# Layer-0 output stage of a two-layer state-space network: quarter-image pieces in two buffers per scan direction, norm weights folded into the projection, inverse root applied to the projected result

## The reference, cut to what matters

```python
y = ys[:, 0] + ys[:, 2, :, ::-1]                      # rows forward + rows backward
yt = ys[:, 1] + ys[:, 3, :, ::-1]                     # columns forward + columns backward
y = y + swapaxes(yt.reshape(B, 384, W, H), 2, 3).reshape(B, 384, L)
mu, var = y.mean(axis=1), y.var(axis=1)               # over the 384 channels
y = (y - mu) * rsqrt(var + 1e-5) * ln_w + ln_b
out = einsum('bdhw,md->bmhw', y, out_proj_w)          # 384 -> 192, then + x
```

## Time and profile before

| | us |
|---|---|
| median of 3 runs | 30645.63 |
| lowest, highest run | 30641.72, 30652.83 |
| the profiled execution, its own time | 30641.48 |
| its span (first to last instruction) | 30639.7 |
| layer-0 output stage, adds of the first image alone | 115.3 |
| the same, from the first mean of image 0 to that of image 7 | 978.5 |
| the same, last image | 98.0 |

### The profile page before, as it was taken

The page is one execution under the profiler, slowest core; times in us unless marked ns, Lnnn a source line. Parts: engine busy times, 40 slices in busy tenths (PEclk is TensorE's granted clock), DMA queues, the critical chain, the costliest instruction groups (busy, mean ns, idle before and its releaser), DMA issues. The chain is left out here.

```text
span 30639.7 us, 217449 instructions
## 1 busy us (share of the span) xinstructions
PE 24095.3 (79%) x57214; PEld 9165.7 (30%) x57214; DVE 26756.3 (87%) x22439; ACT 16129.4 (53%) x26407; POOL 24333.7 (79%) x10344
## 2 busy tenths in 40 slices
PE   8777777777777777777777777775699888888877
PEld 3222222222222222222222222222244322222222
DVE  8899999999999999999999999995411599999984
ACT  2455555555555555555555555553222455555552
POOL 1699999999999999999999999994100466666652
PEclk9899999999999999999999999998899999999998
DMA  6433333333333333333333333335522444444455
GB/s 208 172 132 134 132 133 134 132 134 130 134 134 133 133 132 133 134 133 133 133 132 134 134 132 134 132 133 199 176 74 74 142 166 165 166 166 167 166 172 184
DMA packets 1141977, 4379.93 MB, mean 143 GB/s; under 512 B 251344, under 2 KB 289248, under 8 KB 775392
## 3 DMA queue, kind: packets, MB, share of 16 engines
q1 hardware_dynamic: 1034832, 4016.81, 36.0%
q10 hardware_dynamic: 105904, 349.22, 3.2%
HBM read 3706.94 MB, written 658.64 MB: 142 GB/s over the span
## 5 line engine op out<-in xcount | busy, mean ns | idle before, releaser
L794 POOL TENSOR_TENSOR s_dbu<-s_du,s_b_sb 128x1536 f32<-128x1536 f32 (+1 forms) x5634 | 19172.1, 3404 | 1463.7 <-DVE s_h L856 1437.5
L856 DVE TENSOR_TENSOR_SCAN s_h<-s_dA,s_state,s_dbu 128x512 f32<-128x512 f32 x15296 | 18641.1, 1264 | 621.8 <-ACT s_dA L721 615.5
L721 ACT ACTIVATE s_dA<-s_delta,s_negA 128x512 f32<-128x512 f32 x15360 | 10325.9, 685 | 6095.6 <-DVE s_h L856 6080.2
L596 PE MATMUL s_y_ps<-s_hc,s_ident 128*128 128x512 f32 x22528 | 10818.9, 603 | 0.6 <-DVE s_hc L866 0.5
L866 DVE TENSOR_TENSOR s_hc<-s_h,s_c_ps 128x1024 f32<-128x1024 f32 x5632 | 6721.1, 1193 | 251.3 <-issue 229.3
L803 POOL TENSOR_TENSOR s_hc_pool<-s_h,s_c_sb 128x512 f32<-128x512 f32 x4096 | 6675.4, 1630 | 1.1 <-DVE s_h L856 0.8
L586 PE MATMUL s_c_ps<-s_bc,s_sel 96*128 96x512 bf16 x7168 | 2556.1, 392 | 4957.8 <-DVE s_hc L866 4953.3
L596 PEld LDWEIGHTS s_y_ps<-s_hc,s_ident 128*128 128x128 f32 x22528 | 4389.9, 195 | 3497.6 <-issue 3189.0
L604 PE MATMUL s_y_ps<-s_hc_pool,s_ident 128*128 128x512 f32 x8192 | 4223.5, 597 | 0.0
L586 PEld LDWEIGHTS s_c_ps<-s_bc,s_sel 96*128 96x128 bf16 x7168 | 574.9, 97 | 8719.2 <-DVE s_hc L866 8191.2
L811 POOL TENSOR_TENSOR s_du<-s_delta,s_u 128x1536 f32<-128x1536 f32 (+1 forms) x450 | 1219.5, 2710 | 2431.5 <-ACT s_delta L708 2380.6
(11 more groups left out here) (142 smaller groups left out, 13767.1 us busy)
## 6 DMA issues: line engine op xcount, KB each, us to landing
s_b_sb<-rows SPq DMA_DIRECT2D x1794, 1024.0 KB, 4.7
s_c_sb<-rows SPq DMA_DIRECT2D x1024, 1024.0 KB, 6.2
s_u<-U SPq DMA_DIRECT2D x257, 768.0 KB
Y<-s_yo ACTq DMA_DIRECT2D x256, 768.0 KB, 3.3
m_y<-Y SPq DMA_DIRECT2D x192, 1024.0 KB, 7.5
s_u<-U SPq DMA_DIRECT2D x193, 256.0 KB
U<-f_row SPq DMA_DIRECT2D x24, 2048.0 KB, 17.3
U<-f_col SPq DMA_DIRECT2D x24, 2048.0 KB, 7.1
```

What stands on the lines that cost most here:

```text
L596: last = pe.matmul(y_ps[:, t, :], ident[:, :], hc[:, s % 2, j, :], start=False, stop=s == NS - 1 and j // nd == ng - 1)
L721: act.activation(dA[:, n % DECAYS, :], delta[g % 2][:, t, :], ACT.Exp, scale=negA[g % 2][:, a:a + 1]).then_inc(dA_ready, 1)
L794: pool.tensor_tensor(dbu[:, s % AHEAD, :, :], a, b, ALU.mult).then_inc(dbu_ready, 1)
L856: dve.tensor_tensor_scan(h[:, s % (2 * GROUP), j, :], dA[:, (n * J + j) % DECAYS, :], dbu[:, s % AHEAD, j, :], initial, ALU.mult, ALU.add) ...
```

## The change

* Pieces of 1024 columns (a quarter tile, 512 KB) instead of 2048, and two buffers per direction instead of one, each with its own arrival semaphore. A piece's load now waits until the piece two before it of that direction is used up. Per image that is 12 row adds and 12 column adds on VectorE instead of 6 and 6, 12 adds on GpSimd instead of 6, and 48 loads instead of 24.
* Order of the loads: all four row pieces of a tile (directions 0 and 2), then its four column pieces (1 and 3).
* `w_scaled` = `w_out` times `ln_w`, and `bias` = `w_out` times `ln_b`, are made once at the start of the stage. ScalarE's `affine` and the buffer `yn` are gone; TensorE projects the centred chunk directly, one step earlier: mean(c), variance(c-1), project(c-1).
* The inverse root multiplies the projection's result in PSUM (96x1024) instead of the centred chunk (128x1536). `residual` adds result, bias and `x` in two instructions of 96x512.
* VectorE's slot becomes: centre(c), the due adds (2 or 3 of 24), scale(c-1), residual(c-1). centre(c) waits for project(c-2) instead of affine(c-2); scale(c-1) waits for project(c-1).

Below, longer blocks of removed lines, which stand in the listing above, and unchanged lines are left out.

```diff
-        yk = [sb(f"y{k}", [128, L // 2]) for k in range(K0)]
+        yk = [sb(f"y{k}", [128, 2, LQ]) for k in range(K0)]
         ysum = sb("ysum", [128, 2, ND0, L])
         xin = sb("xin", [HALF, 2, 2, T])
         cen, sq = sb("cen", [128, 2, ND0, T]), sb("sq", [128, ND0, T])
-        yn = sb("yn", [128, ND0, T])
         lnv, rstd = sb("lnv", [128, T]), sb("rstd", [128, T])
         res = sb("res", [HALF, 2, 2, T])
-        ones, w_out = sb("ones", [128, 128]), sb("w_out", [128, ND0, CH])
-        ln_w, ln_b, eps = sb("ln_w", [128, ND0]), sb("ln_b", [128, ND0]), sb("eps", [128, 1])
+        ones, w_out, w_scaled = sb("ones", [128, 128]), sb("w_out", [128, ND0, CH]), sb("w_scaled", [128, ND0, CH])
+        ln_w, ln_b, eps, bias = sb("ln_w", [128, ND0]), sb("ln_b", [128, ND0]), sb("eps", [128, 1]), sb("bias", [HALF, 2])
         mean_ps, var_ps, out_ps = pb("mean_ps", [128, 2, T]), pb("var_ps", [128, 2, T]), pb("out_ps", [HALF, 2, 2, T])
...
-        def over_images(eng, body):
-            for b in range(B):
-                body(b, b % 2)
+        def piece(b, t, part):
+            return (b * ND0 + t) * QUARTERS + part
+        def arrived(eng, k, n):
+            eng.wait_ge(y_in[k][n % 2], (n // 2 + 1) * 16)
         @block.sync
         def _(sp):
...
+            def load(b, k, t, part, free):
+                n = piece(b, t, part)
+                wait(sp, free, n - 1)
+                at = part if k < 2 else QUARTERS - 1 - part
+                sp.dma_start(yk[k][:, n % 2, :].rearrange("p (c j) -> p c j", j=T),
+                             Yv[b, k, t][:, at * CQ:(at + 1) * CQ, :]).then_inc(y_in[k][n % 2], 16)
+            for b in range(B):
                 for t in range(ND0):
-                    for hf in range(2):
-                        for k in (0, 2, 1, 3):
-                            load(b, k, t, hf)
-            over_images(sp, image)
+                    for part in range(QUARTERS):
+                        load(b, 0, t, part, rows_added)
+                        load(b, 2, t, part, rows_added)
+                    for part in range(QUARTERS):
+                        load(b, 1, t, part, cols_added)
+                        load(b, 3, t, part, back_added)
...
+            for half in range(2):
+                for t in range(ND0):
+                    last = pe.matmul(out_ps[:, 0, half, 0:1], w_out[:, t, half * HALF:(half + 1) * HALF],
+                                     ln_b[:, t:t + 1], start=t == 0, stop=t == ND0 - 1)
+            last.then_inc(bias_done, 1)
+            pe.wait_ge(weights_ready, 2)
...
-                wait(pe, rstd_ready, m - 1)
+                wait(pe, lnv_ready, m - 1)
...
             def project(b, c):
-                pe.wait_ge(yn_ready, m + 1)
+                pe.wait_ge(cen_ready, m + 1)
                 wait(pe, res_ready, m - 1)
                 for half in range(2):
                     for t in range(ND0):
-                        last = pe.matmul(out_ps[:, c % 2, half, :], w_out[:, t, half * HALF:(half + 1) * HALF],
-                                         yn[:, t, :], start=t == 0, stop=t == ND0 - 1)
+                        last = pe.matmul(out_ps[:, c % 2, half, :], w_scaled[:, t, half * HALF:(half + 1) * HALF],
+                                         cen[:, c % 2, t, :], start=t == 0, stop=t == ND0 - 1)
                 last.then_inc(out_done, 1)
             def image(b, q):
-                pe.wait_ge(cols_done, (b + 1) * 2 * ND0)
-                for c in range(NCHUNK + 2):
+                pe.wait_ge(cols_added, (b + 1) * ND0 * QUARTERS)
+                for c in range(NCHUNK + 1):
                     if c < NCHUNK:
                         mean(b, q, c)
-                    if 1 <= c <= NCHUNK:
+                    if c:
                         variance(b, c - 1)
-                    if c >= 2:
-                        project(b, c - 2)
...
-            def image(b, q):
-                for c in range(NCHUNK + 3):
+            def image(b):
+                for c in range(STEPS):
                     if c < NCHUNK:
                         squares(b, c)
+                    if c >= 2:
+                        store(b, c - 2)
+                    if c < NCHUNK:
+                        load_x(b, c)
                     if 1 <= c <= NCHUNK:
                         root(b, c - 1)
...
         @block.vector
         def _(dve):
             dve.memset(eps[:, :], LN_EPS).then_inc(eps_set, 1)
...
+            dve.wait_ge(const_in, 64)
+            for t in range(ND0):
+                last = dve.tensor_scalar(w_scaled[:, t, :], w_out[:, t, :], ln_w[:, t:t + 1], None, ALU.mult)
+            last.then_inc(weights_ready, 1)
+            dve.wait_ge(bias_done, 1)
+            dve.tensor_copy(bias[:, :], out_ps[:, 0, :, 0]).then_inc(weights_ready, 1)
+            dve.wait_ge(weights_ready, 2)
+            def add_rows(b, t, part):
+                n = piece(b, t, part)
+                arrived(dve, 0, n)
+                arrived(dve, 2, n)
+                wait(dve, mean_done, (b - 1) * NCHUNK)
+                dve.tensor_tensor(ysum[:, b % 2, t, part * LQ:(part + 1) * LQ], yk[0][:, n % 2, :], yk[2][:, n % 2, ::-1],
                                   ALU.add).then_inc(rows_added, 1)
...
+            def add_columns(b, t, part):
+                n = piece(b, t, part)
+                dve.wait_ge(rows_added, piece(b, t, QUARTERS))
+                dve.wait_ge(back_added, n + 1)
+                some = ysum[:, b % 2, t, :].rearrange("p (h w) -> p h w", w=W)[:, :, part * WQ:(part + 1) * WQ]
+                dve.tensor_tensor(some, some, yk[1][:, n % 2, :].rearrange("p (w h) -> p h w", h=H),
+                                  ALU.add).then_inc(cols_added, 1)
             def centre(b, q, c):
                 m = b * NCHUNK + c
                 dve.wait_ge(mean_done, m + 1)
-                wait(dve, yn_ready, m - 1)
+                wait(dve, sq_ready, m - 1)
+                wait(dve, out_done, m - 1)
                 dve.tensor_tensor(cen[:, c % 2, :, :], ysum[:, q, :, c * T:(c + 1) * T],
                                   mean_ps[:, c % 2, :].unsqueeze(1).broadcast_to([128, ND0, T]),
                                   ALU.subtract).then_inc(cen_ready, 1)
             def scale(b, c):
-                m = b * NCHUNK + c
+                m = b * NCHUNK + c
+                dve.wait_ge(out_done, m + 1)
                 dve.wait_ge(rstd_ready, m + 1)
-                dve.wait_ge(sq_ready, m + 1)
-                dve.wait_ge(cen_ready, m + 1)
-                dve.tensor_tensor(cen[:, c % 2, :, :], cen[:, c % 2, :, :],
-                                  rstd[:, :].unsqueeze(1).broadcast_to([128, ND0, T]), ALU.mult).then_inc(scaled, 1)
+                dve.tensor_tensor(out_ps[:, c % 2, :, :], out_ps[:, c % 2, :, :],
+                                  rstd[0:HALF, :].unsqueeze(1).broadcast_to([HALF, 2, T]), ALU.mult).then_inc(scaled, 1)
             def residual(b, c):
                 m = b * NCHUNK + c
-                dve.wait_ge(out_done, m + 1)
+                dve.wait_ge(scaled, m + 1)
                 dve.wait_ge(x_in[c % 2], b * (16 * NCHUNK // 2) + (c // 2 + 1) * 16)
                 wait(dve, stored[c % 2], b * (16 * NCHUNK // 2) + (c // 2) * 16)
-                dve.tensor_tensor(res[:, c % 2, :, :], out_ps[:, c % 2, :, :], xin[:, c % 2, :, :],
-                                  ALU.add).then_inc(res_ready, 1)
-            STEPS = NCHUNK + 2
+                for half in range(2):
+                    last = dve.scalar_tensor_tensor(res[:, c % 2, half, :], out_ps[:, c % 2, half, :], bias[:, half:half + 1],
+                                                    xin[:, c % 2, half, :], ALU.add, ALU.add)
+                last.then_inc(res_ready, 1)
+            def add(b, step):
+                t, part = divmod(step, 2 * QUARTERS)
+                if part < QUARTERS:
+                    add_rows(b, t, part)
+                else:
+                    add_columns(b, t, part - QUARTERS)
+            ADDS = ND0 * 2 * QUARTERS
             def image(b, q):
                 for c in range(STEPS):
                     if c < NCHUNK:
                         centre(b, q, c)
+                    if not is_last(b):
+                        for step in range(c * ADDS // STEPS, (c + 1) * ADDS // STEPS):
+                            add(b + 1, step)
                     if 1 <= c <= NCHUNK:
                         scale(b, c - 1)
...
+                        residual(b, c - 1)
+            for step in range(ADDS):
+                add(0, step)
+            for b in range(B):
+                image(b, b % 2)
         @block.gpsimd
         def _(pool):
-            def image(b, q):
+            for b in range(B):
                 for t in range(ND0):
...
+                    for part in range(QUARTERS):
+                        n = piece(b, t, part)
+                        arrived(pool, 1, n)
+                        arrived(pool, 3, n)
```

(56 more changed lines are left out.)

19 lines of the change are left out of this document (6 added, 13 removed).

## The result

The changed kernel takes 30492.68 us (median of 5 runs, 30485.75 to 30495.48) against 30645.63: ratio 0.9949, 95% interval [0.9935, 0.9964]. That is 153 us less; forecast were 202 less (30443, range 30350 to 30535). The profiled execution has a span of 30493.7 us, 146.0 less than before. The stage itself goes from 1191.7 us (20899.50 to 22091.20) to 1042.4 (20895.59 to 21938.02), 149.3 less; the rest of the program, where no instruction was changed, took 3.3 us more in this execution.

The account below looks back on a forecast made before the run. The stage was taken as bound by a chain of waits, loads waiting for their single buffers, with no engine full. Gains of 16 + 181 + 5 = 202 us gave 30443 us, range 30350 to 30535 for 8 in 10.

Parts of the forecast that it names:

- image 0, first load to first mean: Image 0's adds without chunk work: three tiles of 30.6 us each, ending at 97.3 us instead of 113.5, gain 16.
- period: One image with chunks, walked through VectorE's slots: 113.9 us against 139.8, gain 181 us over seven.
- rival B: Loads: half-size transfers hold the channel as long as whole ones; period 173 us, total about 30905 us; chance 0.03.
- the prediction's sign: Loads: GB/s in full stretches below 300 would show the forecast wrong, in favour of rival B.
- x and x1 beside the chunks: Loads beside chunks: x and x1 add about 0.3 us per pair (3.0) and 0.5 us per release to use (6.1).
- Durations: Single operations: row add 1.2 us, column add 1.92, GpSimd add 2.35, scale in PSUM 1.22, residual 1.48, centre 1.75.
- the GpSimd hold: A GpSimd add that meets a VectorE add counts as starting when that ends; worth some 1 to 2 us per image.
- the places of the stalls: TensorE inside an image: 1.8 us lost at centre(3) and its square, 3.2 us at centre(7) with a bit in slot 5.
- Rival C: VectorE's short-run column adds don't shrink, 3.7 us each; period 136, total about 30610 us; chance 0.05.
- D: Rival: contention of small transfers and locks costs 1.5 us more at each of 8 waits; period 126, 30534; chance 0.10.
- Rival A: Loads are hidden and TensorE bounds the stage; period 94.0, total 30280 us; chance 0.12, halfway cases included.
- The start's products: Stage start: 3 products, 12 one-column matmuls and a copy are hidden before the first pieces, at worst 1 us.

Follow-up runs that it names:

- without x: Changed kernel with x loaded only for the first two chunks of image 0, later chunks adding an old x: 30445.61 us, one run.
- x twice: Changed kernel with x loaded a second time for every chunk into a spare tile that nobody reads: 30550.49 us, one run.
- adds early: Changed kernel with its 24 adds spread over slots 0 to 8 instead of 0 to 9: 30549.93 us, ratio 0.9970.
- three buffers: Changed kernel with three buffers of 1024 columns per direction instead of two: 30338.54 us, ratio 0.9901 against the kernel before.
- the halves: Against the kernel before, only the new loads and adds: 30597.77 us, ratio 0.9984; only the new chunk path: 30586.20 us, ratio 0.9981.

## Why the prediction was right or wrong

The time lay in the stated range, the sign and mechanism were right, and the size was a third above the measured one (202 us forecast, 153 measured), because two terms of the period were too small. By its own terms:

| term | forecast | measured |
|---|---|---|
| image 0, first load to first mean | 97.3 | 97.1 |
| period | 113.9 | 121.4 |
| last image, to its last residual | 88.3 | 89.1 |
| gain | 16 + 181 + 5 | 16.3 + 128.5 + 4.4 |

A period splits without rest into three parts on TensorE: its own products, its waits for the square (or the scaled chunk), and the turn, its wait for the next image's last add. The forecast's parts are 8.3 + 77.3 us less the 0.8 of wait in the fill; 0.8 + 5.0; 23.3.

| us per period | products | waits inside | turn | period |
|---|---|---|---|---|
| forecast | 84.8 | 5.8 | 23.3 | 113.9 |
| changed kernel | 88.3 | 8.9 | 24.3 | 121.4 |
| without x | 86.8 | 4.3 | 22.4 | 113.5 |
| x twice | 89.7 | 16.4 | 24.5 | 130.7 |
| adds early | 93.3 | 19.3 | 18.7 | 131.3 |
| three buffers | 85.4 | 0.8 | 16.0 | 102.2 |

* *Image 0: right to 0.2 us.* The walk holds add by add: the last add of the first tile ended 36.3 us after the first load, for 36.1. Smaller errors of either sign cancel in it: release to use was 5.1 us (20919.85 to 20924.92) and not 5.6, and two pairs of 512 KB followed each other after 2.6 us (first uses 20903.08 and 20905.69) to 3.3 (20909.46 and 20912.79), for 2.7. With that rival B (small transfers don't shrink) falls. The 286 GB/s of the whole stretch are an average with pauses; the prediction's sign was the rate in full stretches, and there it is above 300:

```profile
20911.00:20913.00 2.00, 0.00 (x0) 0.00 (x0) 0.20 (x1) 0.00 (x0) 0.00 (x0) 0.50 1.04 390
```

* *The period: two terms, of about the same size.* The first is the mis-sized one, x and x1 beside the chunks. The prediction added 0.3 us per pair and 0.5 us per release. Measured at the three third adds inside the image shown, release to use was 7.45, 7.9 (21286.63 to 21294.54) and 7.6 us (21322.68 to 21330.26) instead of 6.1; in the turn, where no x is loaded, 5.4 and 6.6. With it the waits inside came out 3.1 us and the turn 1.0 us longer than forecast. The second was put at nothing: 77.3 us of work per image is TensorE at full clock, though the forecast itself had gaps in it. The products took 88.3 us instead of 84.8, and with three buffers, where hardly a gap is left, the same 1344 matmul records took 85.4. So some 3 of the 7.5 us are products at a lower clock behind the gaps. The prediction knew this cost from the start of an image (7.5 us instead of 5.1) and did not charge it behind its own gaps. That the kernel without x meets the forecast's 113.9 us to half a microsecond is luck: its parts miss by +2.0, -1.5 and -0.9, and the forecast had an allowance for x in it.
* *Durations, the GpSimd hold, the turn (24.4 for 23.3), the places of the stalls: right.* Rival C falls (1.93 us), and D holds in kind: contention of 1.4 to 1.8 us above the forecast, seen at three waits of the image shown, not at eight.
* *Rival A:* TensorE doesn't bound this kernel; with three buffers it comes near (102.2 us, of which 85.4 are its products), and there the channel or the chain of pieces still costs time.
* *The start's products* ended at 20901.84, before the first row add at 20903.08: hidden.
* Unforeseen: that the halves gain 11 us a period when their separate gains are added and 18 together, and how much hangs on which adds stand in a slot.

VectorE's timeline in the turn of the changed kernel, last column adds:

```profile
21342.74 1.90 DVE L1070 TENSOR_TENSOR m_ysum<-m_ysum,m_y 128x1024 f32<-128x1024 f32 x1
21348.04 1.90 DVE L1070 TENSOR_TENSOR m_ysum<-m_ysum,m_y 128x1024 f32<-128x1024 f32 x1 [3.40 <-POOL m_y L1134]
21353.65 1.90 DVE L1070 TENSOR_TENSOR m_ysum<-m_ysum,m_y 128x1024 f32<-128x1024 f32 x1 [3.70 <-POOL m_y L1134]
```

5.3 and 5.6 us from add to add, load and GpSimd's add in between; the forecast had 5.8 and 4.6.

The Trainium skill's rule in "DMA: Bandwidth & Descriptors", section "Measured (HBM→SBUF, 128 partitions, SWDGE, issued from GpSimd)", to batch transfers to at least 1 MiB, would have spoken against this change. The runs part it in two. With the new chunk path, 1 MB pieces in one buffer give a period of 133.0 us; 512 KB pieces (in the new order of loads) give 189.4 with one buffer, 121.4 with two and 102.2 with three. With two buffers the buffers' bytes are those of one 1 MB piece, and the period is still shorter: the size of a piece alone doesn't decide. 1 MB pieces in two buffers were not run, so what part of the third buffer's gain is more bytes, and what part more pieces, stays open.

## What to carry to other kernels

Where a load waits for its buffer, count the waits from release to use and how many pieces are ahead, not the bytes per transfer; here halving the pieces paid only with the halves used as two buffers. Moving an add to another slot moves waits between the inside of the image and the turn, so add up both. In such a chain charge other transfers of the stretch nearer their whole time on the channel than a share of it, and charge TensorE's slower products behind each gap that the forecast itself has. And before a change in two parts is judged by one of them, look whether each part leaves the other's wait in place.

## What the runs showed of the hardware

* Loads of x of 3.15 MB per period lengthened the period by 7.9 and 9.2 us with two buffers and by 8.0 with three, near their own channel time of 8.1 us each time, at DMA shares of 0.72 to 0.87. Between 1.4 and 2.7 us of that are TensorE's products getting slower.
* The same 1344 matmul records took 85.4 us per period with 0.8 us of waits inside the image (granted clock 0.92 over the stretch) and 93.3 us with 19.3 us of such waits (0.85).
* A GpSimd add that starts during a VectorE add of two SBUF tiles is held until that ends (4.15 us instead of 2.35, so held 1.8 us, with 1.9 us left of VectorE's add).
* A product in place in PSUM (96x1024, 1.22 us) costs VectorE what reading PSUM and writing SBUF costs, and the column add with runs of 16 elements about as much per element as that with runs of 32 (1.93 us for 1024 elements, 3.68 for 2048: 1.9 and 1.8 ns each).
